# A turned weight chain, x added by an accumulating DMA, and x1 rounded a batch later, in an mLSTM cross-attention and MX feed-forward kernel

## The reference

```python
x = x + mlstm(layernorm(x), ctx, ctx, Wi, bi, Wf, bf, ln_scale)   # 16 heads of 32
# mlstm: C = (q k^T / sqrt(32)) * D, D from cumulated log-sigmoid gates and row maxima,
#   h = (C / (max(|sum C|, exp(-max)) + 1e-6)) v, every head normed over its 32 values, times ln_scale
x = x + mx_linear(silu(mx_linear(n, w_gate)) * mx_linear(n, w_up), w_down)   # n = layernorm(x)
# mx_linear rounds activations and weights in blocks of 32 along the contracted axis:
#   a shared power of two from the block's largest value, then a 6- or 4-bit float grid
```

## Time and profile before

| | |
|---|---|
| median of three runs | 545.32 us (544.28 to 547.44) |
| the profiled execution, its own time | 548.92 us |
| its span, first to last instruction | 547.0 us |
| mean granted TensorE clock | 0.877 |
| busy: TensorE / its weight load / VectorE | 449.5 / 299.6 / 434.3 us |
| busy: ScalarE / GpSimd | 243.2 / 249.9 us |

### The profile page before, as it was taken

How to read it: one execution, slowest core, us unless ns; L and a number is a source line. 1 busy time by engine, 2 the same in 40 slices (tenths; PEclk the granted TensorE clock), 3 DMA queues, 4 the chain that set the end, 5 groups by cost and what they waited for, 6 DMA issues and landing times.

```text
span 547.0 us, 10343 instructions
## 1 busy us (share of the span) xinstructions
PE 449.5 (82%) x3465; PEld 299.6 (55%) x3465; DVE 434.3 (79%) x615; ACT 243.2 (44%) x341; POOL 249.9 (46%) x228
## 2 busy tenths in 40 slices
PE   0697988399778686959789698799799999999993
PEld 0597988168556465657658384344344444444441
DVE  5569886679798897979789876798978888888781
ACT  1656663246354363726264464244344434434431
POOL 2444541232553537264644564755334353354443
PEclk9997885579978797987859577799989999999999
DMA  7455621143231413141420203011111111111211
GB/s 225 155 185 168 224 98 38 42 120 116 84 114 59 140 59 120 24 146 48 131 67 20 77 2 116 1 38 40 38 40 40 68 47 38 38 38 39 76 38 38
DMA packets 30566, 43.73 MB, mean 80 GB/s; under 512 B 6980, under 2 KB 11972, under 8 KB 30532
## 3 DMA queue, kind: packets, MB, share of 16 engines
q1 hardware_dynamic: 27280, 42.80, 23.8%
q10 hardware_dynamic: 3252, 0.46, 0.5%
HBM read 34.41 MB, written 8.85 MB: 79 GB/s over the span
## 4 chain that ended last, share of the span: by engine, by line
PE 42%; issue 18%; POOL 17%; DVE 13%; ACT 4%; DMA 3%; POOLq 1%; SPq 0%; DVEq 0%; ACTq 0%
PE psA L1359 8%; PE psA L1368 8%; PE psC L1386 7%; PE psC L1193 4%; POOL early L615 3%; PE psB L1378 3%; PE psA L1256 2%; PE psC L1236 2%; DMA early<-in_x_dram 2%; POOL wq L552 2%; POOL kTa L678 2%; POOL xc L648 2%; PE psA L1165 2%; DVE qTa L1128 2%; DVE pam L941 2%
## 5 line engine op out<-in xcount | busy, mean ns | idle before, releaser
L678 POOL TENSOR_TENSOR kTa<-kTa,ps 128x1024 bf16<-128x1024 bf16 x32 | 62.0, 1937 | 100.8 <-DVE kTa L1131 100.8
L1284 PE MATMUL psA<-vp,DC 128*128 128x128 f32 x512 | 72.4, 309 | 12.1 <-DVE DC L1035 12.1
L1284 PEld LDWEIGHTS psA<-vp,DC 128*128 128x128 f32 x512 | 70.1, 223 | 14.1 <-issue 14.1
L552 POOL TENSOR_TENSOR wq<-wq,ws 128x1024 bf16<-128x1024 bf16 x24 | 50.6, 2108 | 51.9 <-DVE wq L969 51.9
L1359 PE MATMUL psA<-WgT,qTa 128*128 128x512 bf16 x256 | 64.7, 399 | 2.5 <-ACT hf L823 2.5
L1368 PE MATMUL psA<-WuT,qTa 128*128 128x512 bf16 x256 | 63.1, 391 | 1.2 <-DVE kTa L1119 1.2
L1386 PE MATMUL psC<-WdT,kTa 128*128 128x512 bf16 x256 | 60.5, 379 | 2.4 <-ACT kTa L888 2.4
L888 ACT ACTIVATE kTa<-psB 128x1024 bf16<-128x1024 bf16 x32 | 32.8, 1024 | 58.1 <-PE psB L1378 57.9
L1119 DVE TENSOR_TENSOR kTa<-kTa,psA 128x1024 f32<-128x1024 f32 x32 | 39.0, 1219 | 19.4 <-PE psA L1368 19.4
L1035 DVE SCALAR_TENSOR_TENSOR DC<-psA,DC 128x512 f32<-128x512 f32 x64 | 41.0, 684 | 13.5 <-ACT DC L814 10.7
L814 ACT ACTIVATE DC<-psB 128x512 f32<-128x512 f32 x64 | 37.2, 597 | 20.1 <-PE psB L1270 19.6
(11 more groups left out here) (132 smaller groups left out, 857.8 us busy)
## 6 DMA issues: line engine op xcount, KB each, us to landing
early<-in_x_dram SPq DMA_DIRECT2D x16, 512.0 KB, 4.0
wraw<-in_L_ffn_w_down_dram SPq DMA_DIRECT2D x8, 512.0 KB, 5.6
early<-in_ctx_dram SPq DMA_DIRECT2D x8, 512.0 KB, 4.8
wraw<-in_L_ffn_w_gate_dram SPq DMA_DIRECT2D x8, 512.0 KB, 4.3
wraw<-in_L_ffn_w_up_dram SPq DMA_DIRECT2D x8, 512.0 KB, 3.4
x_scratch<-early SPq DMA_DIRECT2D x8, 512.0 KB, 3.0
kTa<-x_scratch SPq DMA_DIRECT2D x16, 256.0 KB, 2.7
out_dram<-kTa SPq DMA_DIRECT2D x16, 256.0 KB, 2.0
```

The lines of the kernel that those rows point to most:

```text
L552: nc.gpsimd.tensor_tensor(blocks(wq[p][:, :]), blocks(wq[p][:, :]), spread(ws4[p][:, :], UB), ALU.mult).then_inc(wq_ready.sem, 1)
L678: nc.gpsimd.tensor_tensor(blocks(pd[h]), blocks(pc[h]), spread(ps4[h][:, :], PB), ALU.mult).then_inc(pq_ready.sem, 1)
L1284: last = nc.tensor.matmul(psA[:, j, to:to + P], DC[n % DCN][:, i4 * P:(i4 + 1) * P], values[:, left:left + P], start=i4 == 0, stop=c == 0, ...
```

## The change

- The weight chain is turned by a unit: w_front of unit 10 and w_round of unit 9 are done before the first step, and each step rounds the gate unit of the *next* batch before c_mult 4, and the up unit of the next batch at its end, ahead of x1_stats. TensorE and ScalarE move their transposes and copies to match.
- `residual` writes ln_scale times the normed heads straight into `x1`, then GpSimd issues a DMA that adds x to it in SBUF. x's own load (`load_xr`) and the buffer `xr` go. `x_added` replaces `x1_ready`.
- x1_norm, x1_round, back_x and the transpose of a batch come one step later than before. In the feed-forward stage the rounding of batches 6 and 7 is cut into three pieces (`x1_amax`, `x1_scale`, `x1_clamp`: lines of the old x1_round) between pairs; x_transpose of 6 and 7 move to tiles 5 and 9.
- The first half tile (`first_half`) goes to `psB` and `psC` and is issued before the last copy of heads; its silu is in ScalarE's last attention step. The last power is split over two chunks and moved behind the first back_p's.
- The very last half tile is cut in two (`tail`): clamp, back_p, transposes and copies by halves, the second half's back_p, its copy and the final scale-and-add on VectorE.
- In the gate stage w_transpose of unit 7 moves behind the gates' transposes, and ScalarE's copy of unit 6 behind the gates' copy.

```diff
-                    sp.wait_ge(y_ready.sem, y_ready.unit(2 * b + B + 2))
-                    settle(sp)
-                    load_gate(b + 2)
-                if not first:
-                    store_x1(b - 1)
-                    load_xr(b)
-                if weights:
                     sp.wait_ge(y_ready.sem, y_ready.unit(2 * b + B + 3))
                     settle(sp)
                     load_up(b + 2)
+                if not first:
+                    store_x1(b - 1)
 
...
             def residual(b):
-                hn = sq.rearrange("p c h d -> p c (h d)")
+
                 gp.wait_ge(hn_ready.sem, hn_ready.at(b, 1))
-                ch.link(nc.gpsimd.tensor_tensor(hn, hn, lns[:, :].unsqueeze(1).broadcast_to([P, NCH, E]), ALU.mult))
-                gp.wait_ge(xr_ld, 16 * b + 16)
                 gp.wait_ge(x1_st, 16 * b + 16)
                 gp.wait_ge(xn_ready.sem, xn_ready.at(b, 0))
                 settle(gp)
-                nc.gpsimd.tensor_tensor(x1, hn, xr, ALU.add).then_inc(x1_ready.sem, 1)
+                nc.gpsimd.tensor_tensor(x1, sq.rearrange("p c h d -> p c (h d)"),
+                                        lns[:, :].unsqueeze(1).broadcast_to([P, NCH, E]), ALU.mult).then_inc(scaled.sem, 1)
+                gp.wait_ge(scaled.sem, scaled.at(b, 1))
+                settle(gp)
+                gp.dma_start(x1, x_v[b], accum_op=ALU.add).then_inc(x_added, 16)
 
...
             def step(b, p, n, first, last):
+                second = isinstance(b, int) and b == 1
+                w_back(2 * b + B + 1, 1)
                 if not first:
                     head_rsqrt(b - 1)
+                if not (first or second):
+                    back_x(b - 2)
                 if not first:
                     residual(b - 1)
                 if not last:
+                    w_back(2 * b + B + 2, 0)
                     carry_q(b + 1, 1 - p)
-                w_back(2 * b + B + 1, 1)
+                    weigh(b + 1, 1 - p)
                 if not first:
                     x1_rsqrt(b - 1)
-                if not last:
-                    w_back(2 * b + B + 2, 0)
-                    weigh(b + 1, 1 - p)
-                if not first:
-                    back_x(b - 1)
 
             w_back(B - 1, 1)
+            w_back(B, 0)
             weigh(0, 0)
...
-            last_power(B - 1)
             back_p(0, 0)
             back_p(0, 1)
-            residual(B - 1)
+            last_power(B - 1, 0)
             back_p(1, 0)
+            last_power(B - 1, 1)
             back_p(1, 1)
             add_x1(0, 0, 0)
-            x1_rsqrt(B - 1)
             back_p(2, 0)
             back_p(2, 1)
             add_x1(1, 1, 0)
             back_p(3, 0)
-            back_x(B - 1)
+            residual(B - 1)
             back_p(3, 1)
+            back_x(B - 2)
             add_x1(2, 0, 1)
-            with gp.Fori(0, TILES // 2 - 2) as i:
+            for t in range(4, 8):
+                back_p(t, 0)
+                back_p(t, 1)
+                if t == 4:
+                    x1_rsqrt(B - 1)
+                if t == 6:
+                    back_x(B - 1)
+                add_x1(t - 1, (t - 1) % 2, (t - 1) // 2)
+            with gp.Fori(0, TILES // 2 - 5) as i:
                 for p in range(2):
                     for h in range(2):
-                        back_p(2 * i + 4 + p, h)
-                    add_x1(2 * i + 3 + p, 1 - p, i + 1 + p)
-            add_x1(TILES - 1, 1, TILES // 2 - 1)
...
             def step(b, p, n, first, last):
-                evac_gate_up(2 * b + B, 0, b)
-                if not first:
-                    head_power(b - 1)
+                second = isinstance(b, int) and b == 1
+                if not (first or second):
+                    x1_norm(b - 2)
                 copy_h(b, p, 0)
                 exps(b, 4)
                 exps(b, 5)
+                if not first:
+                    head_power(b - 1)
+                if not last:
+                    round_const(2 * b + B + 2, 0)
+                evac_gate_up(2 * b + B + 1, 1, b)
                 copy_v(b, p, 1)
-                if not first and not (isinstance(b, int) and b == 1):
-                    evac_xq(b - 2)
                 copy_state(b, p)
                 exps(b, 6)
                 exps(b, 7)
-                if not last:
-                    round_const(2 * b + B + 2, 0)
-                if not first:
-                    x1_norm(b - 1)
+                if last:
+                    act.preload_act_table_set("silu_and_others")
                 copy_h(b, p, 1)
-                evac_gate_up(2 * b + B + 1, 1, b)
-                if not last:
+                if last:
+                    evac_xq(b - 2)
+                    silu(0, 0, first=True)
+                else:
                     exps(b + 1, 0)
                     exps(b + 1, 1)
+                    round_const(2 * b + B + 3, 1)
                     copy_v(b + 1, 1 - p, 0)
                     exps(b + 1, 2)
                     exps(b + 1, 3)
                 square(b, p)
+                if not (first or second or last):
+                    evac_xq(b - 2)
                 if not last:
-                    round_const(2 * b + B + 3, 1)
+                    evac_gate_up(2 * b + B + 2, 0, b + 1)
 
             round_const(B + 1, 1)
+            evac_gate_up(B, 0, 0)
             for k in range(HPC):
                 exps(0, k)
             pipeline2(ch, act, step)
 
-
...
             w_round(B, 0)
             w_pow(B + 1, 1)
+            w_front(B + 2, 0, B // 2 + 1)
+            w_round(B + 1, 1)
...
             def step(b, p, n, first, last):
+                second = isinstance(b, int) and b == 1
+                more = not (isinstance(b, int) and b >= B - 2)
                 for k in range(HPC):
-                    c_mult(b, k)
-                if not first:
-                    head_var(b - 1, 1 - p)
-                if not last:
-                    w_front(2 * b + B + 2, 0, b + B // 2 + 1)
-                w_round(2 * b + B + 1, 1)
-                if not first:
-                    head_norm(b - 1, 1 - p)
-                for k in range(HPC, 2 * HPC):
                     c_mult(b, k)
                 if not last:
                     w_pow(2 * b + B + 2, 0)
                 if not first:
-                    x1_stats(b - 1)
+                    head_var(b - 1, 1 - p)
+                if not (first or second):
+                    x1_round(b - 2)
+                if not first:
+                    head_norm(b - 1, 1 - p)
+                if not last:
+                    w_round(2 * b + B + 2, 0)
+                for k in range(HPC, 2 * HPC):
+                    c_mult(b, k)
                 if not last:
                     w_front(2 * b + B + 3, 1, b + B // 2 + 1)
-                    w_round(2 * b + B + 2, 0)
+                    w_pow(2 * b + B + 3, 1)
+                if more:
+                    w_front(2 * b + B + 4, 0, b + B // 2 + 2)
+                if not last:
+                    w_round(2 * b + B + 3, 1)
                 if not first:
-                    x1_round(b - 1)
-                if not last:
-                    w_pow(2 * b + B + 3, 1)
-
-            pipeline(ch, ve, step)
-            head_var(B - 1, 1)
+                    x1_stats(b - 1)
+
+            pipeline2(ch, ve, step)
 
 
...
+            pair(0, 0, first=True)
             pair(0, 1)
-            head_norm(B - 1, 1)
+            head_var(B - 1, 1)
             pair(1, 0)
             pair(1, 1)
+            x1_amax(B - 2, fch)
+            pair(2, 0)
+            head_norm(B - 1, 1)
+            pair(2, 1)
+            x1_scale(B - 2, fch)
+            pair(3, 0)
+            x1_clamp(B - 2)
+            pair(3, 1)
+            pair(4, 0)
             x1_stats(B - 1)
-            pair(2, 0)
-            pair(2, 1)
-            pair(3, 0)
-            x1_round(B - 1)
-            pair(3, 1)
-            with ve.Fori(0, TILES // 2 - 2) as i:
+            pair(4, 1)
+            pair(5, 0)
+            pair(5, 1)
...
             def step(b, p, n, first, last):
-                w_transpose(2 * b + B, 0, rows_order)
                 for k in range(HPC):
                     heads(b, p, k)
                 decay(b, p, 4)
                 decay(b, p, 5)
+                w_transpose(2 * b + B + 1, 1, rows_order)
                 centre(b, 1)
                 qk(b, 1)
-                if b >= 2:
-                    pe.wait_ge(wT_ev.sem, wT_ev.unit(2 * b + B))
-                    x_transpose(b - 2)
                 state(b)
                 decay(b, p, 6)
                 decay(b, p, 7)
                 for k in range(HPC, 2 * HPC):
                     heads(b, p, k)
                 inter(b, p)
-                if b >= 2:
-                    pe.wait_ge(xqT_ev.sem, xqT_ev.at(b - 2, 1))
-                w_transpose(2 * b + B + 1, 1, rows_order)
                 if not last:
                     decay_qk(b + 1, 1 - p)
                     centre(b + 1, 0)
```

(54 more changed lines are left out.)

198 lines of the change are left out of this document (130 added, 68 removed).

## The result

The changed kernel takes 587.8 us (median of 4 runs, 586.4 to 590.9) beside 545.9 for the kernel before (544.3 to 547.4 in the same session): a ratio of 1.077, 95% interval 1.074 to 1.080. It is slower, as forecast, but by 42 us and not 15, and above my range's end of 573.

What follows compares the result with a forecast made beforehand. VectorE was taken as nearly the bound in attention, busy 26.0 of 30 us. Terms 5.5 + 20.5 - 1.5 - 6 - 3.4 = +15.1 gave 564 profiled, 560.4 as median; likeliest range 550 to 572, 8 in 10 522 to 573.

Steps and rivals of the forecast that it cites:

- The steady step: Attention, batches 2 to 6: 34.5 us a step (18.4 + 16.1) against 30.4, +20.5 over five steps.
- the port's three waits: Steady step's first half: VectorE loses 1.2, 1.9 and 2.36 us to GpSimd's w_back, back_x and residual, which exclude it.
- The constant: Steady step's second half: w_round's rounding constant comes behind exps 1 of the next batch on ScalarE, making it 16.1 us.
- the picture of the prediction: VectorE and GpSimd exclude each other on some instructions; the waiting one gets in first between two back-to-back VectorE instructions.
- Batches 0 and 1: Start of attention: w_round's constants and a wait for head_rsqrt cost +5.5 us, between 0 and +7.
- Batch 7 to the first pair, and the end: Attention's last stretch: -1.5 us (+3 to -5); last pair to the end: -3.4 us (-4 to -1).
- The feed-forward part: First to last pair: halved pow and cut-up rounding bring losses from 9.4 to about 3.4 us: -6 (-9 to -2).
- the forecast's 183.8: Feed-forward time from first to last pair after the change: 189.8 us now, less 6.
- The term for the DMA: Adding x by an accumulating DMA: nothing charged, since 15 us before x1_stats cover its landing.
- The slack of 0.75 a half: Feed-forward: VectorE has 5.82 us a half tile less about 5.05 for a pair, room for inserted pieces.
- a sign of being wrong: Forecast refuted if x1_stats waits for the DMA, or if c_mult 4 follows c_mult 0 within 15 us.
- The faster rival: Attention: GpSimd's waits fall where VectorE does not need it; step 27.5 us, total 520; chance 0.27.

Runs made afterwards that it cites:

- e9: The changed kernel with GpSimd's lns multiply and back_x cut to 64 of 1024 columns, the remaining work left out: 558.3 us, ratio 1.023.
- e3: The changed kernel with ScalarE's rounding constant for a step's second w_round moved ahead of the copy of the second heads: 565.3 us, ratio 1.037.
- e5: e3 with GpSimd's order changed to w_back of the down weights, residual, back_x instead of back_x, residual, w_back: 574.4 us, ratio 1.054.
- e1: The changed kernel with SyncE's store of batch 7's x1 moved behind the output stores and x1 loads of tiles 0 to 3: 580.5 us, ratio 1.059.
- e7: The changed kernel with x loaded by SyncE and added by GpSimd again, no accumulating DMA: 582.7 us, ratio 1.069.
- e13: e1 with VectorE's passes for batches 6 and 7 between the pairs cut to 64 or 128 columns, remaining results left out: 569.8 us.
- e14: e1 with GpSimd's inserted instructions for batches 6 and 7 cut to 1 column of 16 and 64 of 1024: 578.1 us.
- e15: e1 with both cuts, VectorE's passes as in e13 and GpSimd's instructions as in e14: 568.1 us.
- e11: The kernel before with the cut last half tile, the pow in halves and later, batch 7's head work later and SyncE's x1 store later: 552.1 us, ratio 1.008.
- e10: e9's small GpSimd instructions with e3's early constant as well, work left out: 544.1 us, ratio 0.995.
- e2: The changed kernel with the first w_round of a step moved from behind head_norm to behind c_mult 4 to 7: 568.6 us, ratio 1.036.

## Why the prediction was wrong

- **The steady step: right.** 35.0 against 34.5, c_mult 4 at 18.05 to 18.5 (18.4), the second half 16.1 to 17.6 (16.1), w_pow 1.77 (1.9), TensorE's wait 6.15 ("over 6"), VectorE's wait for the constant 3.5 ("some 3"). Two details were off. back_x does not get in before w_round, it gets in before head_norm (2.92), where it starts 0.07 earlier. And the port's three waits are 1.1, 1.7 and 1.9, 4.7 together and not 5.5; small waits in VectorE's queue make up for most of it, so the 18.4 is in part luck. e9 confirms the 3.6 of the last two. The constant cost more than I had in the sum: e3 gives back 3.6 a step, where 16.1 is 2.9 above the 13.2 of VectorE's queue. Heads at the 1.2 GHz level took 6.59, where I had 5.44. The Trainium skill (SBUF — State Buffer, "Who interferes with whom") says of VectorE's two-port modes that the one who issues first has the pair for the whole instruction. w_pow's 1.77 and, in e5, 4.18 agree with exclusion, if w_pow runs in such a mode, which no run shows. But in e5 both back_x, listed 0.03 after w_pow, and carry_q behind it seem to have gone first: w_pow ends 0.55 after carry_q. So neither the listed start nor having waited tells who is next there, and the picture of the prediction, that the one who waits gets in first, is no general rule either.
- **Batches 0 and 1: too low by 2.6** (+8.1, above the bound of +7). e3 gives 7.5 of it back, so it is the constant in both steps; for batch 1 I had put only +1, and it was +2.8, for batch 0 4.5, and it was 5.3.
- **Batch 7 to the first pair, and the end: right** in sign, off by 1 each.
- **The feed-forward part: this step failed.** It said: "Losses come to about 3.4 instead of 9.4: -6". The losses were 23. Without what lies over the forecast's 183.8, 19.9 in all, the time would be some 568 us (587.8 less 19.9, an estimate), inside the range. Five runs split it.
  1. SyncE's store ahead of the x1 loads, 7.3 (e1). I had priced moving residual by what it does on GpSimd, and did not follow SyncE's queue past it, though the kernel before had the same order. The term for the DMA was put at nothing as well: e7, with the DMA out and the order as it is, takes out the same gap and 5.9.
  2. VectorE's inserted work, 8.0 (e13). The slack of 0.75 a half was right, but I subtracted only "head_var (2.4)" and the rounding in "pieces of at most 1.8". head_norm and x1_stats were left out; and between pairs back_p runs on GpSimd, so that the first piece of the rounding takes 3.4 and head_var 4.0 (e1's rows).
  3. GpSimd's inserted work, 3.3 (e14), counted at nothing. The second and the third together are 12.0 (e15), which leaves 0.6.

  The gap from the second half to the third is 9.0 in the changed kernel, nearly the 9.2 of before: the pow no longer stands there, but head_var does. That the pow was a gain to be had is not borne out in the one later place tried (e11).
- **The accumulating DMA: right in attention** (e7: 35.0 either way), wrong behind it (e7: 5.9 of the pairs). It takes 5.6 us to landing. An estimate by the fit of the Trainium skill (DMA: Bandwidth & Descriptors, "Anatomy of one DMA") is 3.2, and the measurement decides. I had named a wait of x1_stats for the DMA as a sign of being wrong. It comes once, in batch 7's step, where VectorE has nothing to do in between (6.31 us at 364.62), and costs nothing: batch 7 to the first pair is 26.1 in e7 too.
- **The profiled execution.** I carried over that the profile of the kernel before was 3.6 above its median. That of the changed kernel is at its median (587.5 and 587.8), so 3.6 of the miss come from there and from no stage.
- **The range** ended at 573 because the feed-forward term's worst case was -2; it should have been at least the full inserted work. The faster rival's step of 27.5 was close to a true bound (e10: 28.0, with work left out), but nothing in this order reaches it.

## What to carry to other kernels

When a piece of work is moved to a later stage, price it there by the gap it falls into, with the other engine's instructions running beside it, and follow every in-order queue that stands behind its result, DMA issue queues first. When two engines exclude each other and one is over 90% busy, another order helps only where it puts the one's work under instructions of the other that do not take part: here the lns multiply under the c_mult, which read PSUM (e2), but not GpSimd's pieces under w_front and w_pow (e5). Less work at the port helped (e9). And before two good reorderings are combined, follow what each puts behind the other's wait.
